# Statistics of a LayerNorm made ahead of a scan, in a Mamba block with a ternary feed-forward layer

## The reference

```
z = layernorm(x)                       # over the last axis, eps 1e-5, no gain
x = x + tanh(g_xattn) * mamba(ctx, z)
x = x + tanh(g_ffn) * ffn(layernorm(x))

mamba: u = silu(causal_conv4(in_proj_w @ ctx) + conv_b)      # (channel 512, time 512)
       dt_lo, B, C = split(x_proj_w @ u)                     # 16 rows each
       delta = softplus(dt_proj_w @ dt_lo + dt_proj_b)
       h[t] = h[t-1] * exp(delta * A) + delta * u * B        # 16 states for each channel
       y = (sum over states of h * C) + D * u
       out = (y * silu(z)).T
ffn:   w3 @ (silu(w1 @ a) * (w2 @ a)), each input RMS-normed and rounded to 8 bits,
       each weight rounded to -1, 0, 1
```

## Time and profile before

| | |
|---|---|
| median of 3 runs | 740.04 us |
| lowest and highest | 739.11 and 740.69 us |
| span of the profiled execution | 737.0 us |
| what lies around the span, from the median | 3.0 us |
| TensorE busy | 629.0 us (85%) |
| VectorE busy | 635.7 us (86%) |
| ScalarE busy | 591.9 us (80%) |
| GpSimd busy | 559.0 us (76%) |

### The profile page before, as it was taken

How to read it: one execution, slowest core, us unless ns; L and a number is a source line. 1 busy time by engine, 2 the same in 40 slices (tenths; PEclk the granted TensorE clock), 3 DMA queues, 4 the chain that set the end, 5 groups by cost and what they waited for, 6 DMA issues and landing times.

```text
span 737.0 us, 8444 instructions
## 1 busy us (share of the span) xinstructions
PE 629.0 (85%) x2558; PEld 249.8 (34%) x2558; DVE 635.7 (86%) x725; ACT 591.9 (80%) x902; POOL 559.0 (76%) x309
## 2 busy tenths in 40 slices
PE   6555766988678999899989999989897979797997
PEld 3121221534234333334333433333332323233443
DVE  1579979899767999998999999999999999977675
ACT  4577875778678999988989999998797989667873
POOL 2026559787759899988989999898899898976731
PEclk9855876999797999999999999999797979798999
DMA  4299881455952112214421211144121111000000
GB/s 109 68 259 289 294 285 36 126 175 155 309 139 85 30 45 56 63 50 107 104 55 44 54 47 51 50 111 107 44 58 43 44 43 44 15 15 0 16 29 30
DMA packets 38461, 67.85 MB, mean 92 GB/s; under 512 B 10848, under 2 KB 13408, under 8 KB 36240
## 3 DMA queue, kind: packets, MB, share of 16 engines
q1 hardware_dynamic: 38416, 67.31, 31.8%
HBM read 46.32 MB, written 4.46 MB: 69 GB/s over the span
## 4 chain that ended last, share of the span: by engine, by line
DVE 49%; PE 21%; issue 11%; ACT 6%; POOL 6%; DMA 3%; SPq 1%; DVEq 0%; ACTq 0%; POOLq 0%
DVE hb L1132 25%; DVE dbu_ps L1123 13%; PE ring L1568 6%; POOL hb L637 3%; PE y_ps L1546 3%; PE ring L1654 2%; ACT dA L865 2%; DVE h_max L1282 2%; PE du_ps L1533 2%; DVE am L1192 2%; PE ring L1514 2%; PE ring L1495 2%; DMA bc_rep<-bc_scratch 1%; DVE u L1078 1%; PE ring L1471 1%
## 5 line engine op out<-in xcount | busy, mean ns | idle before, releaser
L1132 DVE TENSOR_TENSOR_SCAN hb<-dA,dbu_ps 128x1024 f32<-128x1024 f32 x128 | 292.4, 2284 | 12.9 <-ACT dA L865 3.7
L637 POOL TENSOR_TENSOR hb<-hb,bc_rep 128x2048 f32<-128x2048 f32 x52 | 235.9, 4536 | 63.5 <-DVE hb L1132 52.3
L865 ACT ACTIVATE dA<-dl_rep,a_neg 128x511 f32<-128x511 f32 x252 | 160.8, 712 | 20.0 <-DMA dl_rep<-delta 15.0
L1123 DVE TENSOR_TENSOR dbu_ps<-du_ps,bc_rep 128x1024 f32<-128x1024 f32 x128 | 157.7, 1232 | 17.5 <-PE du_ps L1533 11.3
L1533 PE MATMUL du_ps<-du,sel_q 32*128 32x512 f32 x128 | 82.9, 731 | 52.4 <-DVE dbu_ps L1123 52.4
L1546 PE MATMUL y_ps<-hb,sel_s 128*32 128x512 f32 x512 | 125.5, 636 | 1.7 <-POOL hb L637 1.7
L614 POOL TENSOR_TENSOR h<-h,up_sb 128x1024 f32<-128x1024 f32 x24 | 56.5, 2355 | 16.1 <-ACT up_sb L883 15.7
L1654 PE MATMUL ring<-w3T,hT 128*128 128x512 fp8e4 x256 | 59.8, 379 | 1.5 <-ACT hT L951 1.0
L632 POOL TENSOR_TENSOR hb<-hb,bc_rep 128x1024 f32<-128x1024 f32 x22 | 51.8, 2356 | 8.6 <-DVE hb L1132 8.3
L1546 PEld LDWEIGHTS y_ps<-hb,sel_s 128*32 128x32 f32 x512 | 28.5, 116 | 87.0 <-issue 82.2
L1568 PE MATMUL ring<-w1T,a12T 128*128 128x512 fp8e4 x208 | 54.8, 387 | 2.3 <-DVE x L1261 1.2
(11 more groups left out here) (182 smaller groups left out, 1048.9 us busy)
## 6 DMA issues: line engine op xcount, KB each, us to landing
dl_rep<-delta SPq DMA_DIRECT2D x252, 64.0 KB, 2.0
bc_rep<-bc_scratch SPq DMA_DIRECT2D x32, 256.0 KB, 4.7
h<-in_L_ffn_w_dram SPq DMA_DIRECT2D x8, 1024.0 KB, 7.8
x<-in_L_ffn_w_dram SPq DMA_DIRECT2D x8, 1024.0 KB, 6.6
up_sb<-in_L_ffn_w_dram SPq DMA_DIRECT2D x8, 1024.0 KB, 7.1
xt<-in_x_dram SPq DMA_DIRECT2D x16, 256.0 KB, 3.6
out_dram<-x SPq DMA_DIRECT2D x16, 256.0 KB, 2.1
x<-in_x_dram SPq DMA_DIRECT2D x2, 1024.0 KB, 6.3
```

The source lines that it names most:

```text
L637: g.tensor_tensor(hb[:, s % 4, :, :], hb[:, s % 4, :, :], c_rep(s // 16), ALU.mult)\
L865: ins = a.activation(dA[:, s % 2, i, 1:L], dl[:, 1:L], ACT.Exp, scale=a_neg[:, s % 16, i:i + 1])
L1123: v.tensor_tensor(dbu_ps[:, :, :], du_ps[:, :].unsqueeze(1).to_broadcast([P, 2, L]), b_rep(b)[:, 2 * half:2 * half + 2, :], ALU.mult).then ...
L1132: v.tensor_tensor_scan(hb[:, s % 4, 2 * half:2 * half + 2, :].rearrange("p a l -> p (a l)"), dA[:, s % 2, 2 * half:2 * half + 2, :].rearra ...
```

## The change

Mean and variance of all 16 tiles of z are made on VectorE ahead of the first scan. x is loaded for this once more, in four DMAs of 1 MB, into `w1T`, `w2T`, `w3T` (read as float32) and `g3b`. They stand in SP's list behind the loads of A_log. VectorE does the first batch before the convolution taps, the second and third behind them, the fourth behind `du`. GpSimd makes all 16 scales and biases at once with four operations on 128 x 16, ahead of its loop. What did this in the stages is gone: `z_stats` on ScalarE, `z_rstd` on GpSimd, bn_stats, bn_aggr, `z_var` and `z_bias` on VectorE. `xt` is still loaded and still goes through the SiLU. ScalarE waits for the scales in `silu_z`, and for the read rows before it first writes `w1T`; SP waits for them before it loads `g3b`.

```diff
+        def z_rows(b):
+            if b == B - 1:
+                return g3b[:, :].rearrange("p (t d) -> p t d", d=D)
+            words = (w1T, w2T, w3T)[b][:, :, :].rearrange("p a h -> p (a h)").bitcast(F32)
+            return words.rearrange("p (t d) -> p t d", d=D)
...
+            for b in range(B):
+                sp.dma_start(z_rows(b), x[b].rearrange("(t p) d -> p t d", p=P)).then_inc(ld_z[b], 16)
...
+                        if s == 15:
+                            sp.wait_ge(z_read, KQ)
...
-            def z_rstd(k):
-                pool.wait_ge(zvar, k + 1)
-                g.tensor_tensor(zsc[:, k % 2, 1:2], zsc[:, k % 2, 0:1], half_neg[:, :], ALU.pow).then_inc(zrstd, 1)
+            def z_affine():
+                pool.wait_ge(z_stats, KQ)
+                link(g.tensor_scalar(z_bias[:, :], zmv[:, :, 0], -1.0, 0.0, ALU.mult, ALU.add))
+                link(g.tensor_scalar(z_scale[:, :], zmv[:, :, 1], LN_EPS, 1.0, ALU.add, ALU.mult))
+                link(g.tensor_tensor(z_scale[:, :], z_scale[:, :], half_neg[:, :].to_broadcast([P, KQ]), ALU.pow))
+                g.tensor_tensor(z_bias[:, :], z_bias[:, :], z_scale[:, :], ALU.mult).then_inc(z_scaled, 1)
...
+            z_affine()
             for k in range(KQ):
...
-                        z_rstd(k)
...
-            def z_stats(k):
...
-                a.activation(z_junk[:, :], xt[:, k % 2, :], ACT.Copy, scale=-1.0 / D, accum_out=zmv[:, 0:1]).then_inc(z_mean, 1)
-                act.wait_ge(z_mean, n_sum)
-                a.activation(z_junk[:, :], xt[:, k % 2, :], ACT.Square, bias=zmv[:, 0:1], accum_out=zmv[:, 1:2])\
-                 .then_inc(z_square, 1)
...
+            def silu_z(k):
+                act.wait_ge(z_scaled, 1)
+                act.wait_ge(ld_xt[k % 2], 16 * (k // 2 + 1))
+                a.activation(xt[:, k % 2, :], xt[:, k % 2, :], ACT.Silu, bias=z_bias[:, k:k + 1],
+                             scale=z_scale[:, k:k + 1]).then_inc(z_done, 1)
...
+                        if c == 0:
+                            act.wait_ge(z_read, KQ)
...
+            def z_row_stats(b):
+                dve.wait_ge(ld_z[b], 16)
+                for t in range(ET):
+                    v.bn_stats(zst[:, ET * b + t, :], z_rows(b)[:, t, :]).then_inc(z_read, 1)
+                dve.wait_ge(z_read, ET * (b + 1))
+                for k in range(ET * b, ET * (b + 1)):
+                    v.bn_aggr(zmv[:, k, :], zst[:, k, :]).then_inc(z_stats, 1)
...
             v.tensor_scalar(a_neg[:, :, :], a_neg[:, :, :], -1.0, None, ALU.mult).then_inc(a_done, 1)
+            z_row_stats(0)
             for et in range(ET):
                 for shift in (1, 2):
                     link(conv_tap(et, shift))
                 conv_tap(et, 3).then_inc(conv_done, 1)
+            z_row_stats(1)
+            z_row_stats(2)
...
             v.tensor_tensor(du[:, 0, :], delta[:, 0, :], u[:, 0, :], ALU.mult).then_inc(du_done, 1)
+            z_row_stats(3)
...
-                        z_bias(k)
...
-                        if f < 0:
-                            dve.wait_ge(ld_xt[k % 2], 16 * (k // 2 + 1))
-                            st = mark(v.bn_stats(zst[:, :], xt[:, k % 2, :]))
...
-                            st = mark(v.bn_aggr(zmv[:, :], zst[:, :]))
...
-                        z_var(k)
```

More of the change, by code:

```diff
@@ L178, in flamingo_block @@
         xt = sb("xt", [P, 2, L])
-        zst = sb("zst", [P, 6])
-        zmv = sb("zmv", [P, 2])
+        zst = sb("zst", [P, KQ, 6])
+        zmv = sb("zmv", [P, KQ, 2])
+        z_scale = sb("z_scale", [P, KQ])
+        z_bias = sb("z_bias", [P, KQ])
         z_junk = sb("z_junk", [P, D], BF16)
-        zsc = sb("zsc", [P, 2, 3])
         x1 = sb("x1", [P, XB, ET, D])
@@ L263, in flamingo_block @@
         row_square = sem("row_square")
[L264 to L268, removed]
+        ld_z = [sem(f"ld_z{b}") for b in range(B)]
+        z_read = sem("z_read")
+        z_stats = sem("z_stats")
+        z_scaled = sem("z_scaled")
         z_done = sem("z_done")
@@ L783, in row_stats @@
                     act.wait_ge(fbias, ft - ET + 1)
-                act.wait_ge(z_square, ft)
                 if n_sum > 1:
@@ L790, in row_stats @@
                  .then_inc(row_square, 1)
-            def z_stats(k):
-                n_sum = k - LAG_F + 1
-                if n_sum > 2:
-                    act.wait_ge(row_square, row_sums(n_sum - 1 if by_act(n_sum - 1) else n_sum - 2))
+            def silu_z(k):
+                act.wait_ge(z_scaled, 1)
                 act.wait_ge(ld_xt[k % 2], 16 * (k // 2 + 1))
[L798 to L801, removed]
-                a.activation(z_junk[:, :], xt[:, k % 2, :], ACT.Copy, scale=-1.0 / D, accum_out=zmv[:, 0:1]).then_inc(z_mean, 1)
-                act.wait_ge(z_mean, n_sum)
-                a.activation(z_junk[:, :], xt[:, k % 2, :], ACT.Square, bias=zmv[:, 0:1], accum_out=zmv[:, 1:2])\
-                 .then_inc(z_square, 1)
-            def silu_z(k):
-                act.wait_ge(zbias, k + 1)
-                a.activation(xt[:, k % 2, :], xt[:, k % 2, :], ACT.Silu, bias=zsc[:, k % 2, 2:3],
-                             scale=zsc[:, k % 2, 1:2]).then_inc(z_done, 1)
+                a.activation(xt[:, k % 2, :], xt[:, k % 2, :], ACT.Silu, bias=z_bias[:, k:k + 1],
+                             scale=z_scale[:, k:k + 1]).then_inc(z_done, 1)
             def xproj_evac(b):
@@ L992, in _ @@
                             normalise(f)
-                        if f >= 0:
-                            z_stats(k)
                         if g >= 0:
@@ L1309, in evac_hT @@
                 evac_magic(("hT", ft, 0), hT[:, 0:8, :].rearrange("p a b -> p (a b)"), hT_dve)
-            def z_var(k):
-                if k >= 2:
-                    dve.wait_ge(z_done, k - 1)
-                if k < LAG_F:
-                    v.tensor_scalar(zsc[:, k % 2, 0:1], zmv[:, 1:2], LN_EPS, None, ALU.add).then_inc(zvar, 1)
-                    return
-                dve.wait_ge(z_square, k - LAG_F + 1)
-                v.tensor_scalar(zsc[:, k % 2, 0:1], zmv[:, 1:2], 1.0 / D, LN_EPS, ALU.mult, ALU.add).then_inc(zvar, 1)
-            def z_bias(k):
-                dve.wait_ge(zrstd, k + 1)
-                v.tensor_scalar(zsc[:, k % 2, 2:3], zmv[:, 0:1], zsc[:, k % 2, 1:2], -1.0 if k < LAG_F else 1.0,
-                                ALU.mult, ALU.mult).then_inc(zbias, 1)
             def convolve(m):
@@ L1380, in _ @@
                             hidden_scales(g)
-                        if f < 0:
-                            after(st)
-                            st = mark(v.bn_aggr(zmv[:, :], zst[:, :]))
                         if k >= 1:
                             add_scan(k - 1)
-                        if f < 0:
-                            after(st)
-                        z_var(k)
                         if f < 0:
```

## The result

The changed kernel takes 737.02 us (median of 20 runs, 735.40 to 740.50), the kernel before on the same chip 742.21 us (20 runs, 738.51 to 747.91). The ratio is 0.9925, with a 95% interval of 0.9905 to 0.9945: faster, and within the predicted range. The profiled execution has a span of 733.9 us, where before had 737.0: 3.1 us less. The medians are 5.2 us apart, which is more.

What follows compares the result with a forecast made beforehand. It took VectorE's time, in stages where it never waits, as the bound. Stage gains of 4.7 us less 0.85 at the start gave 3.85: 740.0 to 736.2 us, own range 735.0 to 737.8, with rivals 1 and 2 734.6 to 739.4.

Steps and rivals of the forecast that it cites:

- Start, 0.85: Ahead of the first scan: the first statistics group delays the convolution taps and everything behind them by 0.85 us.
- rival 3: At the start: the four z loads share the DMA engines evenly, the first lands late; 743.8 us if at 22; chance 0.08.
- Rival 1: At the start: z's first rows land within 5.0 us, so the start is free; 735.3 us; chance 0.15.
- k = 1 and 2, 0.5 each, indirect: Stages 1 and 2: without z's rsqrt GpSimd works earlier, and VectorE's L1230 and L1239 end 0.5 us sooner each.
- theory C: Experiments' theory: gains or losses ahead of stage 4 are taken up by transfers of B and C and TensorE's clock.
- k = 4, 0.65: Stage 4: 0.55 us from z's rsqrt no longer preceding the rows' rsqrt on GpSimd, and 0.1 for the bias.
- k = 7, 0.8: Stage 7: VectorE no longer waits for ScalarE's z sums, 0.7 us, with the bias 0.8.
- k = 8 to 12 and 14, 0.18 each: Stages where VectorE never waits: the z variance (0.06) and z bias (0.12) removed, 1.1 us over six stages.
- Rival 2: Indirect gains at k = 1, 2 and 4 meet other waits, chunk loads swallow part of k = 0; 738.1 us; chance 0.24.
- Rival 4: ScalarE's removed 1.7 us a stage bounds more stages than k = 7; put under the forecast's lower end, no own chance.
- A: Experiments' theory: the prediction's sum holds term by term, start pays 0.9 us, stages give about 4.0 back.
- theory B: Experiments' theory: medians differ by more than the profiles because the kernel before loses more time in other executions.

Runs made afterwards that it cites:

- taps_first: Changed kernel with no z statistics ahead of the convolution taps: batches 0 and 1 behind the taps, 2 and 3 behind the first du; 737.40 us.
- after_again: The changed kernel once more, no edit, for a second profile; 736.18 us, ratio 0.9926 to the kernel before.
- pool_kept: Changed kernel with one GpSimd operation (pow on 128x1) put back in each stage where z's rsqrt was, result unread; 738.83 us.
- after_third: The changed kernel, unchanged, profiled a third time; 736.14 us, ratio 0.9901 to the kernel before.
- before_again: The kernel before once more, no edit, for a second profile; 742.14 us, profiled span 744.8 us.
- act_kept: Changed kernel with ScalarE's two passes over xt put back in each stage from stage 4 on, results unread; 738.86 us.
- dve_kept: Changed kernel with two VectorE operations put back in each stage where z_bias and z_var were made, results unread; 740.37 us.
- add_only: Kernel before with only the four loads and the 16 bn_stats and bn_aggr added, results unused; 743.08 us.
- c_first: Changed kernel with g3b's load and one weight chunk moved behind the second batch's broadcast of C; 735.51 us.
- c_first_again: The same kernel as c_first, run once more; 737.32 us.
- both_moves: Changed kernel with the edit of taps_first and the two moved loads of c_first together; 735.87 us.
- no_stats: Changed kernel without any mean or variance of z (scale 1, bias 0) and without their loads; 738.46 us.

## Why the prediction was right, step by step

The signs that the prediction named came: bn_stats at 14.65 (about 14.4), the first tap at 17.46 (17.3), the loss of digits at 33.33 (33.3), a period of 37.31 (37.3) and no wait for z_junk in stage 7.

- **Start, 0.85.** Measured 0.95 at the first tap, and 0.64 to 1.22 at the first scan in three profiles. That it is paid to the end is not shown: taps_first was 2.69 late at the first scan and no later than after_again by (0,1,1). The loads landed after 5.9 us, as taken, and one after the other, so rival 3 is out. They came 2.7 us apart (14.7, 17.4, 20.1, 22.8), where I had taken 4.0, so z was in at 22.8 and not at 26.4. The Trainium skill's page "DMA: Bandwidth & Descriptors" (section Anatomy of one DMA — SWDGE (gpsimd) path) has its fit of 2.0 us plus the bytes by 436 GB/s for DMAs on GpSimd's path, and these are SyncE's, so the trace does not test it. As an estimate by it the first would land after 4.4 us, where the trace has 5.9, and each further megabyte 2.4 us later, near the trace's 2.7.
- **bn_stats and bn_aggr, 0.61 and 0.11 start to start.** Four and four took 2.81 us from 14.65 to 17.46, against 2.95. What the prediction calls the drain is the 0.06 us by which the first bn_aggr starts later than an independent operation would; in the trace it starts 0.04 us after the last bn_stats has ended (17.12 and 17.16). Rival 1 is out: the start was not free.
- **Groups two to four hide.** 1.35 us of the gap was left behind the third and 0.41 behind the fourth. So they cost nothing.
- **k = 0, 0.8.** 1.00 from (0,1,1) to (0,2,0), all that VectorE did there. The chunk load did not limit it.
- **k = 1 and 2, 0.5 each, indirect.** 0.52 each, and shown by pool_kept. But between them 0.75 was lost ahead of (2,1,1), and 0.74 in after_third (in before_again 1.12, so it is no price of the change). The second 0.52 falls in stage 3, between (3,0,0) and (3,0,1), where L1239 stands.
- **k = 3, nothing.** In the profile 1.16 was given back between (3,0,1) and (4,0,0). 0.85 of it lies ahead of (3,2,0), where x's projection takes 5.33 us (granted clock 0.79 from 158 to 166) instead of 3.63. In after_again, the same kernel, it takes 3.63, and 0.82 is gained over the same steps. So this is no price of the change either. The wait for B's broadcast took the rest, and in after_again 1.03: its write to scratch left at 178.17 and 178.32, against 178.19 before, however early the scans were. That is theory C at work. TensorE's timeline, changed kernel and then after_again:

```profile
158.05 5.33 PE L1493 MATMUL ring<-u,w_xT 128*48 128x512 f32 x8
```

```profile
159.29 3.63 PE L1493 MATMUL ring<-u,w_xT 128*48 128x512 f32 x8
```

- **k = 4, 0.65.** 1.1 from (4,1,1) to (5,0,1) in all three profiles, pool_kept 0.32 in its one. Of the 0.8 between them 0.5 lies ahead of (4,2,0), where VectorE's wait behind the rsqrt is 0.51 longer: that is the term as given. The other 0.3, ahead of (5,0,0), has no cause that the runs show.
- **k = 5 and 6, 0.36.** 0.42, of which 0.24 in stage 5.
- **k = 7, 0.8.** 0.82. The cause as given, a wait of VectorE for the accumulators, is shown by act_kept.
- **k = 8 to 12 and 14, 0.18 each.** 0.11, 0.13 (beside the loss below), 0.18, 0.18, 0.29, 0.27, from VectorE's two operations in stages 10 and 11, as dve_kept shows. k = 13 and 15, put at nothing, gave 0.18 and 0.39. Against it stands a loss of 0.6 in stage 9, in all three profiles of the changed kernel, beside a new stretch at half clock (granted 0.64 from 380 to 383 in the first). The two go together in all 14 profiles: seven lose 0.5 to 2.1 between (8,3,1) and (9,1,1) and have a granted clock of 0.64 to 0.89 from 380 to 383, and the other seven (before, before_again, add_only, act_kept, c_first, c_first_again, both_moves) lose nothing there and have 1.00. What sets the clock back is open; the prediction has no term for it.

Stages 5 to 15 together: predicted 2.26, measured 2.33 to 2.34 in the three profiles. That this sum is so close is luck: the loss in stage 9 cancels the 0.57 of stages 13 and 15, which had no term either. Up to (5,0,0): predicted 2.45 less 0.85 = 1.6, measured 0.5 to 1.0. The step that was too large is that early gains add up to the end. Rival 2 said that they don't, and was half right, by another way: they arrive, and the clock and the broadcasts take some of them back. Rival 4 is out for stages 6 to 13, where act_kept gains at least what the changed kernel gains, but not for stage 4.

So A's mechanism holds for stages 6, 7, 10, 11 and 13, C describes what lies ahead of stage 5 apart from the indirect gains of 0.52, and B is what is left for the medians.

**The time, and luck in it.** The 736.2 us were a span of 733.2 plus 3.0 around it. That last term was too large: in all 146 timed executions of the two kernels that have a span on record, 1.7 to 1.9 us lie around it. So the profiled execution of before took some 738.9 us (an estimate, 737.0 + 1.9), less than the 740.0 that the prediction started from, and the median of before came out at 742.2. The measured 737.0 is 0.8 from the forecast because errors cancel: the span came out 0.7 above 733.2, what lies around it 1.1 below 3.0, and the median 1.2 above the profiled execution. The chances given for faster add up to 0.80 and not to 0.77, which changes nothing.

**The medians.** Over all runs the changed kernel's 42 have quartiles of 735.7 and 737.7 and a lowest of 734.1; before's 124 have 739.9 and 744.7, and 737.7. At the lower end the difference is 3.6, near the span's 3.1 and the predicted 3.85. At the upper quartiles it is 7.0. The mean granted clock of an execution goes with this. Of before's 104 executions that have it on record, the 34 with 0.909 or more have a median of 739.5 us, and the 23 such of the changed kernel 736.2: 3.3 apart, as the profiles are. With less than 0.909 the medians are 743.9 (70 executions) and 737.4 (19): 6.5 apart. So before has more executions with a low clock, and loses more in them, which is theory B. What comes first, the lower clock or the later work, these numbers don't say. before_again (granted 0.901) shows one execution of the upper part, and that its time was lost up to stage 4. Part of it, the 2.69 us for z_junk and the GpSimd operation, hangs on what the change removes. That this makes the whole difference of the scatter is argued, not shown: only profiled executions show where their time goes, and there are two of before.

## What to carry to other kernels

Work on the pacing engine is free where that engine waits anyway: here 11.3 us of statistics ahead of the first scan made it start 0.6 to 1.2 us later. What an operation on the critical engine's path is worth is the distance between starts there, and a wait for another engine counts whole: look at what a removed instruction waited for, not only at its duration. One profile fixes a gain of 0.2 us in a stage where VectorE never waits (here 6, 10, 11 and 13, where every profile without the two operations gains 0.17 to 0.20 on before), but not in stages that hang on transfers and on the clock: there take several profiles of the same program before believing a difference of 3 us. And a sum that comes out right can be two errors of opposite sign: compare term by term.

## What the runs showed of the hardware

GpSimd's pow on 128x16 took 2.93 us, where on 128x1 it takes 0.55: 0.16 us a column more. The prediction had taken 0.55 at most. It was hidden, since the first product came at 46.77:

```profile
39.38 0.20 POOL L672 TENSOR_SCALAR z_scale<-zmv 128x16 f32<-128x16 f32 x1
39.67 2.93 POOL L673 TENSOR_TENSOR z_scale<-z_scale,half_neg 128x16 f32<-128x16 f32 x1
42.68 0.22 POOL L674 TENSOR_TENSOR z_bias<-z_bias,z_scale 128x16 f32<-128x16 f32 x1
```

SP's issues took longer behind a backlog. With the four z loads under way those of ctx and xt took 1.77 and 2.55 us; before, and in no_stats without these loads, the same two took 0.39 and 0.51:

```profile
9.86 0.51 SPq L434 DMA_DIRECT2D w3T<-in_x_dram  x1
10.41 0.82 SPq L434 DMA_DIRECT2D g3b<-in_x_dram  x1
12.08 1.77 SPq L497 DMA_DIRECT2D a<-in_ctx_dram  x1
13.89 2.55 SPq L482 DMA_DIRECT2D xt<-in_x_dram  x1
```

And the first x projection, eight matmuls, took 3.6 to 6.6 us in 14 profiled executions of near-identical programs, waits between them left out: 3.60 to 3.81 in seven, 4.96 to 5.36 in four, 6.57 to 6.59 in three. The granted clock from 24 to 28 us was 1.00 in the seven, 0.57 to 0.83 in the four and 0.50 in the three.
